# A graph layer on one Trainium2 core: degree factors folded into the matrix, and two tile pairs prepared during the counts

## The chip, the core and the metric

The kernel runs on one core of a Trainium2 chip. The core has five engines that run their own instruction queues and meet at semaphores: TensorE (matrix products from SBUF into PSUM), VectorE, ScalarE, GpSimd (SBUF only in this kernel) and SyncE, which issues the DMA transfers. The metric is the device time of one execution in microseconds, 912.77 us as the median of three runs (912.65 to 914.29).

## What is computed

`x` is 64 tiles of 128 rows (T) by 1024 nodes (N). The reference, cut to what matters (h = relu(layernorm(x)), n = 1024 nodes):

```python
x_avg = mean of h over the 64 tiles, per node;  x_norm = x_avg / |x_avg|
sim  = (x_norm @ x_norm.T + 1) * 0.5                       # n x n
adj  = (sim + gumbel0 > 1 - sim + gumbel1)                 # n x n, 0 or 1
adj_sym = clip(adj + adj.T, 0, 1); nmask = clip(adj_sym + eye, 0, 1)
common = nmask @ nmask.T;  max_common = common.max()
struct = where(adj_sym * (common > 1) > 0, common / max_common * common, 0)
W = adj * struct;  deg = W.sum(axis=0);  dinv = deg ** -0.5 (0 where deg is 0)
Wn = dinv[:, None] * W * dinv[None, :]
out = einsum('sd,sbt->dbt', Wn, einsum('nbt,to->nbo', h, weight)) + bias
result = x + out, transposed back to the layout of x
```

So the 64 tiles need one matrix Wn that depends on all of them, and then each tile is x + (h W) Wn + bias.

## The kernel before

**First pass (to about 110 us).** All 64 tiles are loaded, normalised and summed; of every eighth tile the product with W is kept (`xw_res`, tile RESIDENT = 0 of each trip).

**Setup (about 110 to 231 us).** TensorE makes sim, the symmetric mask, and the counts `common` in eight chunks of 128 rows, in the order of `CHUNKS`: chunk e of the upper half, then its partner of the lower half (L642 to L652, 16 matmuls each, three PSUM buffers `ps_com`). VectorE multiplies each with the adjacency into `masked[e]` (L859), the square root of W but for constants. ScalarE squares it into `a32(e)` (L426). The degrees are sums over rows of `a32` on TensorE (`degrees`, L618, matmuls one column wide). The matrix is wanted in seven combinations of its four 512 x 512 blocks for a Strassen-like product (Winograd's form, seven half-size products instead of eight), each split into a high and a low fp16 part (`a16[part, matrix 0 to 6]`): VectorE makes the combinations per chunk (`ts`, L812, and t3 on GpSimd, L353), ScalarE the high parts (`high_a`, `high_t`, L413 to L422), VectorE and GpSimd the low parts (L828 to L840, L363). The degree factors are not in `a16`: `dinv` goes into `u` (L899), by which z is multiplied, and into the row factor `row_fb` (L989), by which the results are multiplied. Only then are pair 0's tiles prepared.

**The loop.** 32 pairs of tiles, eight trips of four pairs (`act_pair`, `pe_pair`, `dve_pair`, and a GpSimd loop, L367). Tiles of a pair are the two halves (b = 0, 1) of the seven-product scheme. For the pair after next ScalarE makes h twice, fp32 and fp16 (`relu2`, L446 and L447), and VectorE the low fp16 part (`h_low`, L850). For the next pair TensorE makes h W (`xw_of`, L674, 24 matmuls a tile; the resident tile has none), VectorE turns it into z (`z_of`, L920, times u), GpSimd makes four sums of z (L370 to L375), ScalarE casts z and its sums in four groups to fp16 (`y_high`, L462), and VectorE subtracts for the low parts (`y_low`, L928). For the pair itself TensorE makes seven products of twelve matmuls of 512 columns (`product`, L683) in the order of matrices 0, 3, 4, 2, 5, 1, 6, in three PSUM banks (`ps_a`, `ps_b`, `ps_d`), reusing `ps_b` four times in a row as a running sum. Its intermediate states are copied out by ScalarE (`partial`, L476, four a pair) and combined on VectorE (L956, L962, L966), multiplied by the row factor and the weight's sum (`scale`, L932), and finished with bias and x (`finish`, L939). SyncE stores the tile and reloads its slot of `xring` (L277, L279).

The order on each engine is written by hand, and each engine is in order. In the loop ScalarE's order is: partial 0, y_high 0, partial 1, relu2, partial 2, y_high 1, relu2, y_high 2, partial 3, y_high 3. The last product, matrix 6, waits for partial 3:

```python
pe.wait_ge(s_v, 4 * r + 4)          # L707
product(q, 2, 6, ps_b, False)
```

## Time and profile before

| | |
|---|---|
| median of three runs | 912.77 us (912.65 to 914.29) |
| the profiled execution, its time | 917.18 us |
| its span, first to last instruction | 915.3 us |
| mean granted TensorE clock | 0.978 of full |
| DMA | 109.4 MB, mean 120 GB/s |

The profile names an instruction by engine, line of the kernel and operation, with output and inputs. PE is TensorE's matmul, PEld its weight load, DVE VectorE, ACT ScalarE, POOL GpSimd. An instruction's idle bracket is the time that its engine stood before it, and what released it. A busy TensorE is not TensorE at its peak: its matmuls overlap, so the starts of the runs of matmuls say more than the busy time. fp32 matmuls stand in the trace twice each. The granted clock is given as a share of 2.4 GHz; 0.5 is 1.2 GHz. Ends of matmuls are modelled, and GpSimd's spans are rough.

### The profile page before, as it was taken

The numbers are of one execution on the slowest core, as the hardware profiler recorded it, in microseconds if no ns is written. First come the engines' busy times: TensorE is split into PE (matmuls) and PEld (weight loads), VectorE is DVE, ScalarE is ACT, GpSimd is POOL, SyncE is SP. The second block draws the span as 40 slices with busy tenths as digits, with TensorE's granted clock in tenths as the row PEclk, the third lists the DMA queues.
The fourth block names the chain that finished last, engine by engine and source line by source line (L and its number), as shares of the span: only waits on it lengthen the run. The fifth ranks groups of instructions, "written<-read, shape, count | busy, mean of one in ns | idle before, by whom it ended". The sixth has DMA issues, their size and how long they took to land.

```text
span 915.3 us, 13816 instructions
## 1 busy us (share of the span) xinstructions
PE 846.0 (92%) x4772; PEld 435.1 (48%) x4772; DVE 748.9 (82%) x792; ACT 424.2 (46%) x472; POOL 336.9 (37%) x264
## 2 busy tenths in 40 slices
PE   5999899968999999999999999999999999999997
PEld 3444455654454445444444454444444444444453
DVE  7998666888888888888888888888888888888885
ACT  3888703455444443444344444444444444444431
POOL 4788511254333333333333333333334333433330
PEclk9999899868999999999999999999999999999999
DMA  8999600040222222222222232223222222222112
GB/s 351 409 399 401 278 1 1 1 184 1 92 93 93 92 92 92 92 92 92 106 94 94 94 135 89 98 94 113 92 92 92 92 92 92 92 92 92 47 47 92
DMA packets 29108, 109.40 MB, mean 120 GB/s; under 512 B 3360, under 2 KB 3488, under 8 KB 28064
## 3 DMA queue, kind: packets, MB, share of 16 engines
q1 hardware_dynamic: 29088, 109.13, 32.3%
q8 instruction: 13, 0.21, 0.1%
q14 instruction: 7, 0.06, 0.0%
HBM read 75.56 MB, written 33.55 MB: 119 GB/s over the span
## 4 chain that ended last, share of the span: by engine, by line
DVE 29%; issue 27%; PE 14%; ACT 14%; POOL 13%; DVEq 1%; ACTq 1%; POOLq 1%; DMA 0%; SPq 0%
DVE zbuf L920 8%; DVE obuf L932 7%; DVE obuf L962 5%; POOL zbuf L372 5%; ACT ybuf L462 4%; PE ps L683 4%; POOL zbuf L370 4%; PE ps L650 3%; ACT hring L447 3%; ACT hring L446 3%; DVE ybuf L928 2%; DVE obuf L966 2%; PE ps L555 2%; ACT p L476 1%; PE ps L626 1%
## 5 line engine op out<-in xcount | busy, mean ns | idle before, releaser
L683 PE MATMUL ps<-a,ybuf 128*128 128x512 f16 x2688 | 598.8, 380 | 36.3 <-ACT obuf L476 29.9
L683 PEld LDWEIGHTS ps<-a,ybuf 128*128 128x128 f16 x2688 | 256.6, 98 | 357.4 <-ACT obuf L476 50.5
L462 ACT ACTIVATE ybuf<-zbuf 128x1024 f16<-128x1024 f32 (+1 forms) x128 | 121.6, 950 | 333.3 <-DVE zbuf L920 227.8
L928 DVE TENSOR_TENSOR ybuf<-zbuf,ybuf 128x1024 f16<-128x1024 f32 (+1 forms) x128 | 190.0, 1484 | 60.3 <-ACT ybuf L462 60.3
L370 POOL TENSOR_TENSOR zbuf<-zbuf 128x512 f32<-128x512 f32 x32 | 41.5, 1296 | 455.3 <-DVE zbuf L920 455.3
L850 DVE TENSOR_TENSOR hring<-hring 128x1024 f16<-128x1024 f32 x56 | 73.3, 1308 | 51.3 <-ACT hring L447 51.3
L674 PE MATMUL ps<-w,hring 128*128 128x128 f16 x1344 | 85.5, 221 | 3.6 <-DVE hring L850 3.6
L674 PEld LDWEIGHTS ps<-w,hring 128*128 128x128 f16 x1344 | 79.6, 99 | 18.4 <-DVE zbuf L920 7.4
L476 ACT ACTIVATE obuf<-ps 128x512 f32<-128x512 f32 x96 | 56.2, 586 | 64.3 <-PE ps L683 64.3
L939 DVE SCALAR_TENSOR_TENSOR obuf<-obuf,bias_sb,xring 128x1024 f32<-128x1024 f32 x64 | 82.2, 1285 | 2.9
L375 POOL TENSOR_TENSOR zbuf<-zbuf 128x512 f32<-128x512 f32 x32 | 71.8, 2244 | 0.0
L373 POOL TENSOR_TENSOR zbuf<-zbuf 128x512 f32<-128x512 f32 x32 | 70.9, 2216 | 0.0
L446 ACT ACTIVATE hring<-xring,nbias,rstd 128x1024 f32<-128x1024 f32 x56 | 68.7, 1228 | 0.1
L447 ACT ACTIVATE hring<-xring,nbias,rstd 128x1024 f16<-128x1024 f32 x56 | 68.7, 1227 | 0.0
L920 DVE TENSOR_TENSOR zbuf<-ps,u 128x1024 f32<-128x1024 f32 x56 | 68.2, 1217 | 0.6 <-DVE hring L989 0.4
L932 DVE SCALAR_TENSOR_TENSOR obuf<-obuf,w_sum,hring 128x512 f32<-128x512 f32 x64 | 64.9, 1015 | 1.2
L962 DVE TENSOR_TENSOR obuf<-obuf,p 128x512 f32<-128x512 f32 x32 | 53.8, 1683 | 2.5 <-ACT obuf L476 2.5
L372 POOL TENSOR_TENSOR zbuf<-zbuf 128x512 f32<-128x512 f32 x32 | 51.8, 1620 | 2.5
L748 DVE BATCH_NORM_STATS2 stats<-xring 128x6 f32<-128x512 f32 x64 | 38.9, 671 | 0.7 <-issue 0.7
L748 DVE BATCH_NORM_STATS2 stats<-ybuf 128x6 f32<-128x512 f32 x56 | 34.2, 668 | 3.0 <-DMA ybuf<-in_x_dram 3.0
L555 PE MATMUL ps<-hring,ident 128*128 128x512 f32 x76 | 35.1, 609 | 0.0
L650 PE MATMUL ps<-xring 128*128 128x512 bf16 x128 | 30.7, 400 | 0.0
(142 smaller groups left out, 629.6 us busy)
## 6 DMA issues: line engine op xcount, KB each, us to landing
xring<-in_x_dram SPq DMA_DIRECT2D x96, 512.0 KB, 5.0
out_dram<-obuf SPq DMA_DIRECT2D x64, 512.0 KB, 3.0
ybuf<-in_x_dram SPq DMA_DIRECT2D x28, 512.0 KB, 9.7
a<-in_L_gnn_gumbel_dram SPq DMA_DIRECT2D x7, 1024.0 KB, 14.7
obuf<-in_x_dram SPq DMA_DIRECT2D x4, 512.0 KB, 11.8
...
bias_sb<-in_L_gnn_bias_dram SPq DMA_DIRECT2D x1, 0.5 KB, 2.1
```

Source lines behind the costliest of these rows:

```text
L370: nc.gpsimd.tensor_tensor(z[:, 4, :], z[:, 0, :], z[:, 3, :], ALU.add).then_inc(s_zs, 1)
L372: nc.gpsimd.tensor_tensor(z[:, 5, :], z[:, 4, :], z[:, 1, :], ALU.subtract).then_inc(s_zs, 1)
L446: nc.scalar.activation(h32, xring[:, j, :], ACT.Relu, bias=bias, scale=scale).then_inc(s_h32, 1)
L447: nc.scalar.activation(h16[b][:, 0, :], xring[:, j, :], ACT.Relu, bias=bias, scale=scale).then_inc(s_hhi, 1)
L462: nc.scalar.activation(y16[:, q % 2, 0, a:a + n, :], z[:, a + 1:a + 1 + n, :], ACT.Copy).then_inc(s_yhi, 1)
L674: mm = nc.tensor.matmul(ps_xw2[:, c * P:(c + 1) * P], h16[b][:, hk, c * P:(c + 1) * P], w16[:, wk, :], start=(hk == wk == 0), stop=(hk == ...
L683: mm = nc.tensor.matmul(bank[q % 2], y16[:, q % 2, yk, u, c * P:(c + 1) * P], a16[:, ak, mat, c, :], start=(start and c == yk == ak == 0), ...
L920: nc.vector.tensor_tensor(dst.rearrange("p m (c t) -> p m c t", c=HC), src, u[:].rearrange("p (m c) -> p m c", m=2).unsqueeze(3).broadcast_to(
L928: nc.vector.tensor_tensor(y16[:, q % 2, 1, a:a + n, :], z[:, a + 1:a + 1 + n, :], y16[:, q % 2, 0, a:a + n, :], ALU.subtract).then_inc(s_y, 1)
L932: return nc.vector.scalar_tensor_tensor(out=dst, in0=src, scalar=w_sum[:, 0:1], in1=row_fb[:, cols], op0=ALU.mult, op1=ALU.mult)
L939: nc.vector.scalar_tensor_tensor(out=ob, in0=ob, scalar=bias_sb[:, 0:1], in1=xring[:, j, :], op0=ALU.add, op1=ALU.add).then_inc(s_out, 1)
L962: nc.vector.tensor_tensor(o1[:, HI], o1[:, HI], p5[:], ALU.add).then_inc(s_c22, 1)
```

## The change

Both degree factors go into the matrix. As W is a square, the kernel makes `masked * q_row * q_column` with q = deg^(-1/4), and squares it: the square holds dinv on both sides. So z needs no `u` (a constant scale), and results no row factor. This needs the degrees before the matrix, so the matrix is no longer made chunk by chunk during the counts but after them, in whole blocks of 4 x 512 columns.

- Degrees: TensorE also transposes the adjacency, chunk by chunk (`turn_adj`), ScalarE copies it to SBUF (`turned`), VectorE makes a second, transposed mask of the same counts (`mask_t`), and ScalarE squares it with a sum along the row (`degree_of`). The degree matmuls are gone. GpSimd's powers of -1/4 come in two groups (`roots`, chunks 0 to 5 and 6 to 7).
- Two count buffers in PSUM instead of three.
- During the counts pairs 0 and 1 are prepared (relu2, xw_of, z, z_sums, y_high and most of y_low), from x tiles loaded into free buffers (`x_first`).
- After the counts q is spread over a row in PSUM (`ps_q`, `ps_q2`). VectorE multiplies the upper blocks' chunks (`rooted`), GpSimd the lower blocks' (`rows_lo`, from a copy of the row in SBUF); ScalarE squares all (`square`), with a scale that holds the constants (and for the lower blocks the column factor).
- z_of moves from VectorE to ScalarE. Three partial sums are copied by ScalarE with scale and bias (Identity), the fourth is read by VectorE directly (`upper1`). VectorE's combinations scale in the same pass (`upper0`, `upper1`, `lower0`, `lower1`) and `add_x` adds x.
- The first trip's pairs are written out ahead of the loops; product 6 of a pair waits for `upper1`.
- The loads of the first eight x slots wait for the end of the matrix (`s_t` 3, `s_alo` 5 and 6).

The diff, cut to its core and indented less (of `dve_pair`, at the end, only the lines that stay or come; `MADE` is (0, 3, 2, 4, 5, 1, 6), the order in which the matrices become ready):

```diff
-        sp.wait_ge(s_com, C)
-        sp.wait_ge(s_m, C)
-        for j in (1, 2, 3, 0, 4, 5, 6, 7):
+        sp.wait_ge(s_adj, C)
+        for k, j in enumerate((1, 2, 3)):
+            sp.dma_start(x_first[j], x[j]).then_inc(s_xf[k], 16)
+        sp.wait_ge(s_t, 3)
+        sp.wait_ge(s_alo, 5)
+        for j in (4, 5, 6, 7):
+            sp.dma_start(xring[:, j, :], x[j]).then_inc(s_x2[j], 16)
+        sp.wait_ge(s_alo, 6)
+        for j in (0, 1, 2, 3):
             sp.dma_start(xring[:, j, :], x[j]).then_inc(s_x2[j], 16)
...
+        def roots(n, a, b):
+            pool.wait_ge(s_degmin, 2 * n + 2)
+            nc.gpsimd.tensor_tensor(q_raw[:, a:b], degree_min[:, a:b], neg_quarter[:, a:b],
+                                    ALU.pow).then_inc(s_qraw, 1)
+        pool.wait_ge(s_cnt, 1)
+        nc.gpsimd.tensor_tensor(k0[:, 1:2], k0[:, 0:1], neg_half[:, 0:1], ALU.pow).then_inc(s_k0, 1)
+        z_sums(0)
+        roots(0, 0, 6)
+        z_sums(1)
+        roots(1, 6, C)
+        pool.wait_ge(s_qsb, 1)
+        for c in range(HC):
+            nc.gpsimd.tensor_tensor(rows_lo[:, c, :], masked[2 * c + 1], q_row, ALU.mult).then_inc(s_elo, 1)
+        pool.wait_ge(s_a32, C)
+        pool.wait_ge(s_t, 1)
+        nc.gpsimd.tensor_tensor(rows_hi[:, :, HI], rows_lo[:, :, HI], rows_hi[:, :, HI],
+                                ALU.subtract).then_inc(s_t3, 1)
+        with pool.Fori(2, TRIPS * PAIRS) as r:
+            z_sums(r)
...
+            dst = z[:, 1:3, :] if b == 0 else z[:, 0:4:3, :]
+            nc.scalar.activation(dst, src, ACT.Copy, scale=Y_SCALE / W_SCALE).then_inc(s_z, 1)
...
+                act.wait_ge(s_c, 4 * r + 6)
+            act.wait_ge(s_mm, 14 + 7 * r + (1, 2, 3)[k])
+            dst = (o[q % 2][0][:, 0:H], p5[:], o[q % 2][0][:, H:N])[k]
+            src = (ps_b, ps_d, ps_b)[k][q % 2]
+            nc.scalar.activation(dst, src, ACT.Identity, bias=bias_sb[:, 0:1],
+                                 scale=w_out[:, 0:1]).then_inc(s_v, 1)
...
         def act_pair(i, q, ahead1, ahead2):
             partial(i, q, 0)
             if ahead1:
+                z_of(i, q + 1, 0)
                 y_high(i, q + 1, 0)
             partial(i, q, 1)
             if ahead2:
                 relu2(i, q + 2, 0)
             partial(i, q, 2)
             if ahead1:
+                z_of(i, q + 1, 1)
                 y_high(i, q + 1, 1)
             if ahead2:
                 relu2(i, q + 2, 1)
             if ahead1:
                 y_high(i, q + 1, 2)
-            partial(i, q, 3)
-            if ahead1:
                 y_high(i, q + 1, 3)
...
+        def degree_of(e):
+            act.wait_ge(s_mt, e + 1)
+            if e >= 2:
+                act.wait_ge(s_deg, e - 1)
+            nc.scalar.activation(square_t[e % 2], masked_t[e % 2], ACT.Square,
+                                 accum_out=degree[:, e:e + 1]).then_inc(s_deg, 1)
...
+        turned(7)
+        degree_of(6)
+        degree_of(7)
+        y_high(0, 1, 2)
+        y_high(0, 1, 3)
+        act.wait_ge(s_qrow, 2)
+        act.wait_ge(s_deg, C)
+        nc.scalar.activation(q_row, ps_q2, ACT.Copy).then_inc(s_qsb, 1)
...
+        for c in range(HC):
+            square(rows_hi, 0, c)
+        act.wait_ge(s_a32, HC)
+        high(0, rows_hi[:, :, LO])
+        square(rows_lo, 1, 0)
+        square(rows_lo, 1, 1)
+        act.wait_ge(s_t, 1)
+        high(3, spare)
+        square(rows_lo, 1, 2)
+        square(rows_lo, 1, 3)
+        act.wait_ge(s_a32, C)
+        high(2, rows_lo[:, :, HI])
+        act.wait_ge(s_t, 2)
+        high(4, rows_hi[:, :, LO])
+        act.wait_ge(s_t3, 1)
+        high(5, rows_hi[:, :, HI])
+        high(1, rows_lo[:, :, LO])
+        act.wait_ge(s_wout, 1)
+        partial(0, 0, 0)
+        partial(0, 0, 1)
+        partial(0, 0, 2)
+        act.wait_ge(s_t, 3)
+        high(6, spare)
+        relu2(0, 2, 0)
+        relu2(0, 2, 1)
...
+        for e, c in enumerate(CHUNKS):
+            if e >= 2:
+                pe.wait_ge(s_m, e - 1)
+                pe.wait_ge(s_mt, e - 1)
+            for k in range(C):
+                if e == 0:
+                    for n in {c % 2, k % 2}:
+                        pe.wait_ge(s_mask[n], max(c, k) // 2 + 1)
+                if e >= 1 and k == HC:
+                    turn_adj(e)
+                for m in range(2):
+                    mm = nc.tensor.matmul(ps_com[e % 2][:, m * H:(m + 1) * H], nmask[:, k, c * P:(c + 1) * P],
+                                          nmask[:, k, m * H:(m + 1) * H], start=(k == 0), stop=(k == C - 1),
+                                          skip_group_check=True)
+            mm.then_inc(s_com, 1)
+            if e == 0:
+                turn(0)
+                turn_adj(0)
+            if e == 1:
+                spread(0)
+                xw_of(0, 0, 1)
+            if e == 3:
+                xw_of(0, 1, 0)
+            if e == 6:
+                xw_of(0, 1, 1)
+        pe.wait_ge(s_m, C)
+        turn(1)
+        pe.wait_ge(s_adjt, C)
+        for dst in (ps_q, ps_q2):
+            for c in range(C):
+                e = CHUNKS.index(c)
+                mm = nc.tensor.matmul(dst[:, c * P:(c + 1) * P], qf[:, e:e + 1].broadcast_to([P, P]), ident[:],
+                                      start=True, stop=True, skip_group_check=True)
+            mm.then_inc(s_qrow, 1)
+            if dst is ps_q:
+                spread(1)
...
-            pe.wait_ge(s_v, 4 * r + 4)
+            pe.wait_ge(s_c, 4 * r + 10)
+            made(6)
             product(q, 2, 6, ps_b, False)
...
+        root(0, 0, 6)
+        y_low(0, 1, 1)
+        bound(1, 6, C)
+        root(1, 6, C)
+        dve.wait_ge(s_q, 2)
+        nc.vector.tensor_reduce(col2[:, 1:2], qf[:], AX_X, ALU.max).then_inc(s_colmax, 1)
...
+        top_of(1)
+        y_low(0, 1, 2)
+        dve.wait_ge(s_qrow, 1)
+        rooted(rows_hi, 0, 0)
+        dve.wait_ge(s_topb, 2)
+        nc.vector.tensor_scalar(q_top[:], ps_top[1][:, P:P + 1], Q_MIN, None, ALU.max).then_inc(s_kap, 1)
+        rooted(rows_hi, 0, 1)
+        dve.wait_ge(s_kap, 1)
+        nc.vector.reciprocal(q_inv[:], q_top[:]).then_inc(s_kap, 1)
+        rooted(rows_hi, 0, 2)
+        dve.wait_ge(s_kap, 2)
+        dve.wait_ge(s_k0, 1)
+        nc.vector.tensor_scalar(kappa[:, 0:1], q_inv[:], k0[:, 1:2], A_SCALE ** 0.5, ALU.mult,
+                                ALU.mult).then_inc(s_kap, 1)
+        dve.wait_ge(s_cnt, 2)
+        nc.vector.tensor_scalar(w_out[:], q_top[:], q_top[:, 0:1], w_count[:, 0:1], ALU.mult,
+                                ALU.mult).then_inc(s_wout, 1)
+        rooted(rows_hi, 0, 3)
+        dve.wait_ge(s_kap, 3)
+        nc.vector.tensor_scalar(kappa_lo, qf[:].rearrange("p (c k) -> p k c", k=2)[:, 1, :], kappa[:, 0:1], None,
+                                ALU.mult).then_inc(s_kap, 1)
+        dve.wait_ge(s_a32, HC)
+        nc.vector.tensor_tensor(spare, rows_hi[:, :, HI], rows_hi[:, :, LO], ALU.subtract).then_inc(s_t, 1)
+        low(0, rows_hi[:, :, LO])
+        low(3, spare)
+        dve.wait_ge(s_a32, C)
+        dve.wait_ge(s_t, 1)
+        dve.wait_ge(s_alo, 1)
+        nc.vector.tensor_tensor(rows_hi[:, :, LO], rows_lo[:, :, HI], spare, ALU.subtract).then_inc(s_t, 1)
+        low(2, rows_lo[:, :, HI])
+        low(4, rows_hi[:, :, LO])
+        dve.wait_ge(s_t, 2)
+        dve.wait_ge(s_alo, 2)
+        nc.vector.tensor_tensor(spare, rows_lo[:, :, LO], rows_hi[:, :, LO], ALU.subtract).then_inc(s_t, 1)
+        low(5, rows_hi[:, :, HI])
+        low(1, rows_lo[:, :, LO])
...
+        def upper1(i, q):
+            r, ob = PAIRS * i + q, o[q % 2][1]
+            dve.wait_ge(s_mm, 14 + 7 * r + 5)
+            dve.wait_ge(s_v, 3 * r + 2)
+            nc.vector.scalar_tensor_tensor(out=ob[:, HI], in0=ps_b[q % 2], scalar=w_out[:, 0:1], in1=p5[:],
+                                           op0=ALU.mult, op1=ALU.add).then_inc(s_c, 1)
+        def add_x(i, q, b):
             j, ob = 2 * q + b, o[q % 2][b]
+            dve.wait_ge(s_c, 8 + 4 * (PAIRS * i + q) + 3 + b)
             dve.wait_ge(s_x2[j], 16 * (i + 1))
-            nc.vector.scalar_tensor_tensor(out=ob, in0=ob, scalar=bias_sb[:, 0:1], in1=xring[:, j, :],
-                                           op0=ALU.add, op1=ALU.add).then_inc(s_out, 1)
...
         def dve_pair(i, q, ahead1, ahead2):
             if ahead1:
                 y_low(i, q + 1, 0)
             if ahead2:
                 h_low(i, q + 2, 0)
             if ahead1:
                 y_low(i, q + 1, 1)
+            upper0(i, q)
             if ahead2:
                 h_low(i, q + 2, 1)
+            upper1(i, q)
             if ahead1:
                 y_low(i, q + 1, 2)
+            lower0(i, q)
+            add_x(i, q, 0)
             if ahead1:
                 y_low(i, q + 1, 3)
+            lower1(i, q)
+            add_x(i, q, 1)
...
+        upper0(0, 0)
+        low(6, spare)
+        upper1(0, 0)
+        y_low(0, 1, 3)
+        h_low(0, 2, 0)
+        lower0(0, 0)
+        add_x(0, 0, 0)
+        h_low(0, 2, 1)
+        lower1(0, 0)
+        add_x(0, 0, 1)
+        for q in range(1, PAIRS):
```

## Rows read from the trace of the kernel before

**Rows 1.** The page, busy time by engine over the whole span.

```profile
PE 846.0 (92%) x4772; PEld 435.1 (48%) x4772; DVE 748.9 (82%) x792; ACT 424.2 (46%) x472; POOL 336.9 (37%) x264
```

**Rows 2.** Timeline of PE, one pair: start us, duration us, instruction, count, idle bracket.

```profile
506.23 8.09 PE L683 MATMUL ps<-a,ybuf 128*128 128x512 f16 x36
515.64 5.35 PE L683 MATMUL ps<-a,ybuf 128*128 128x512 f16 x24 [1.32 <-ACT obuf L476]
520.83 1.50 PE L674 MATMUL ps<-w,hring 128*128 128x128 f16 x24
522.17 5.34 PE L683 MATMUL ps<-a,ybuf 128*128 128x512 f16 x24
527.35 1.50 PE L674 MATMUL ps<-w,hring 128*128 128x128 f16 x24
528.89 18.30 PE L683 MATMUL ps<-a,ybuf 128*128 128x512 f16 x84
```

**Rows 3.** Timeline of all engines in the same pair, ahead of the idle bracket.

```profile
509.68 1.22 DVE L920 TENSOR_TENSOR zbuf<-ps,u 128x1024 f32<-128x1024 f32 x1
...
512.41 1.61 POOL L372 TENSOR_TENSOR zbuf<-zbuf 128x512 f32<-128x512 f32 x1
...
512.80 0.68 DVE L956 TENSOR_TENSOR obuf<-ps,obuf 128x512 f32<-128x512 f32 x1
...
514.05 1.06 ACT L462 ACTIVATE ybuf<-zbuf 128x1024 f16<-128x1024 f32 x1 [0.23 <-POOL zbuf L372]
515.01 0.58 ACT L476 ACTIVATE obuf<-ps 128x512 f32<-128x512 f32 x1
515.13 2.22 DVE L928 TENSOR_TENSOR ybuf<-zbuf,ybuf 128x1024 f16<-128x1024 f32 x1
...
517.28 1.75 DVE L962 TENSOR_TENSOR obuf<-obuf,p 128x512 f32<-128x512 f32 x1
```

**Rows 4.** Timeline of PE, pair 0 and the start of pair 1.

```profile
212.29 7.72 PE L683 MATMUL ps<-a,ybuf 128*128 128x512 f16 x24 [4.00 <-DVE ybuf L928]
221.19 13.11 PE L683 MATMUL ps<-a,ybuf 128*128 128x512 f16 x60
```

**Rows 5.** Timeline of all engines, the end of the run.

```profile
880.81 28.65 PE L683 MATMUL ps<-a,ybuf 128*128 128x512 f16 x132
...
910.94 1.28 DVE L939 SCALAR_TENSOR_TENSOR obuf<-obuf,bias_sb,xring 128x1024 f32<-128x1024 f32 x1
```

**Rows 6.** Groups by line and form: busy us, mean ns of one | idle us before.

```profile
L462 ACT ACTIVATE ybuf<-zbuf 128x1024 f16<-128x1024 f32 x96 | 101.5, 1057 | 274.4 <-DVE zbuf L920 168.9 <-POOL zbuf L375 89.2 <-POOL zbuf L372 11.6
...
L446 ACT ACTIVATE hring<-xring,nbias,rstd 128x1024 f32<-128x1024 f32 x56 | 68.7, 1228 | 0.1
...
L932 DVE SCALAR_TENSOR_TENSOR obuf<-ps,w_sum,hring 128x512 f32<-128x512 f32 x32 | 23.9, 745 | 0.0
...
L422 ACT ACTIVATE a<-obuf 128x2048 f16<-128x2048 f32 x4 | 7.6, 1898 | 1.0 <-DVE obuf L823 1.0
...
L839 DVE TENSOR_TENSOR a<-obuf,a 128x2048 f16<-128x2048 f32 x2 | 4.6, 2291 | 2.4 <-ACT a L422 2.4
```

**Rows 7.** Timeline of PE in the setup: four of the counts, and the row factor's spread.

```profile
153.18 13.99 PE L650 MATMUL ps<-xring 128*128 128x512 bf16 x64
...
201.32 3.04 PE L536 MATMUL ps<-ident,row_f 128*128 128x128 f32 x16
```

**Rows 8.** Timeline of all engines after the counts, 189 to 200 us.

```profile
189.44 2.10 POOL L360 TENSOR_TENSOR dinv_raw<-degree,neg_half 128x8 f32<-128x8 f32 x1 [2.73 <-DVE has_deg L885]
...
191.51 6.14 POOL L363 TENSOR_TENSOR a<-obuf,a 128x1024 f16<-128x1024 f32 x2
...
194.53 4.20 DVE L850 TENSOR_TENSOR hring<-hring 128x1024 f16<-128x1024 f32 x1
```

**Rows 9.** Windows: busy us (instructions) by engine, then granted clock, DMA share, GB/s.

```profile
190.00:200.00 10.00, 2.17 (x15) 1.80 (x16) 9.24 (x13) 2.40 (x2) 7.64 (x3) 0.50 0.60 245
```

**Rows 10.** One line's instructions: durations in ns, first and last start in us.

```profile
L397 ACT ACT_TABLE_LOAD  x1: 1283/1283/1283, 0.8 to 0.8; - x1
```

More of the change, by code:

```diff
@@ L48 @@
 Y_SCALE = 256.0
+A_SCALE = 2.0 ** 14
+Q_MIN = 1e-6
 def gnn_kernel(nc, x, adj, bias, gumbel, out):
@@ L992, in _ @@
+            lower0(0, 0)
[3 more added lines that the diff above has]
+            add_x(0, 0, 1)
+            for q in range(1, PAIRS):
+                dve_pair(0, q, True, True)
+            with dve.Fori(1, TRIPS - 1) as i:
                 for q in range(PAIRS):
```

475 lines of the change are left out of this document (218 added, 257 removed).

## The prediction, made before the changed kernel was run

> **What bounds the kernel now.** I read the page's first part first [rows 1]: TensorE is busy 92% of the span, VectorE 82%, ScalarE and GpSimd under half. Busy time says little of a pipelined matmul, so the next view is TensorE's timeline in one pair of the steady loop [rows 2]. The reader is to see the starts there: 24 product matmuls from 515.64 to 520.83, 5.19 us, is 0.216 us each; the 24 matmuls of one tile's x·W take 1.34 us when nothing holds them (520.83 to 522.17). A pair of tiles has 84 product matmuls and two x·W, so it needs 18.14 + 2.68 = 20.82 us. It takes 22.66 us (506.23 to 528.89). The hole is at 515.64: TensorE stood 1.32 us for ScalarE's copy at L476, and 0.2 us more before each second x·W (1.54 instead of 1.34, 527.35 to 528.89) for VectorE's z. Of four pairs in a trip three have the hole.
>
> Which chain ends last at that hole is in the timelines of the other engines [rows 3]: VectorE writes z at 509.68, GpSimd's sums of z follow until 514.0, ScalarE's cast of that sum stands in its queue at 514.05, and only behind it, at 515.01, the copy of the fourth partial sum, on which product 6 of the pair waits (`s_v`, L707). The copy needs nothing of z; it is merely queued behind it. VectorE itself is late with z because it spends some 18 us of each pair's 22.
>
> Products are named here by their matrix, in the order 0, 3, 4, 2, 5, 1, 6 in which a pair runs them. So the loop has a price above TensorE's own work, and the setup ahead of it a long chain. Two anchors divide the run [rows 4, 5]. Five products run without a hole from 221.19 (60 matmuls); four belong to pair 0, so pair 1 starts at 221.19 + 48 x 0.216 = 231.5. The last matmul ends at 880.81 + 28.65 = 909.5, the last VectorE instruction at 910.94 + 1.28 = 912.2, the span at 915.3. The 31 pairs between take 678.0 us.
>
> **The loop.** Removed on VectorE: z_of (two of 1.22), the second reading of c22, three scalings by the row factor, the bias. Added: nothing; upper0, upper1 and lower0 scale and add in one pass from PSUM (0.75 each, by the same form of L932 [rows 6]), lower1 0.7, add_x twice 1.22 (the width of z_of in [rows 3]). y_low 4.3 and h_low 2.4 stay. I make it 12.1 us of own time instead of some 18 (82% of 22 [rows 1]), plus one to two us of standing behind GpSimd. Added on ScalarE: z_of twice, 1.0 us each from PSUM; the copy of the fourth partial sum (0.59) goes; the three others get a scale and a bias held in a column each, which in [rows 6] makes 1.228 of 1.057 for 1024 columns, so 0.17 each. The casts 3.8, four copies 2.3 and four relus 4.9 made 11.0; 11.0 + 2.0 - 0.6 + 0.5 = 12.9 us in 20.8, which still fits.
>
> What is late next? With product 0 of a pair starting at 0, x·W ends at 3.9, ScalarE has z at 5.2 and its cast at 6.2; the second x·W ends at 10.5, z at 11.7. GpSimd's four sums then take turns with VectorE's operations until 20.1, and the last cast is out at 21.2, ahead of the next pair's first copy at 23.4. VectorE reads product 5's sum (upper1) as soon as it ends, at 15.6, unless h_low is still before it: h_low waits for relu2, done at 14.7, and perhaps one GpSimd instruction, and ends at 15.9 to 16.5; upper1 then at 17.3 at the latest. Product 6 asks for it at 18.2. So I cost the loop at TensorE's own work, with 0.9 us to spare at the narrowest place. What is queued behind upper1's wait on VectorE is y_low of the next pair, not needed for 7 us. The loads and stores keep their places behind add_x; a result is stored 24 us after its pair's start and its buffer wanted at 44.
>
> Sum of the loop: 31 x 84 x 0.216 = 562.5, and 53 x·W (60 tiles of pairs 2 to 31 less 7 resident ones) at 1.34 = 71.0, together 633.5 against 678.0: **-44.5 us**. It can't gain more, since no matmul is taken away; it can gain less by what new waits arise, bounded by the old hole of 1.32 a pair.
>
> **The end.** The last block had a scaling and the addition behind it; now lower1 (0.7) and add_x (1.23), from 909.5: 911.5 instead of 912.2 [rows 5]. **-0.7 us**.
>
> **The setup.** I carry the time of the trace along. The counts start at 145.8 as before. TensorE now does there 8 counts at 3.46 us (64 matmuls in 13.8 [rows 7]), 8 transposes of eight 128-column matmuls (a third of an x·W, 0.45) and three x·W: 27.7 + 3.6 + 4.0 = 35.3, and with holes of 1.5 us (the two count buffers wait for both masks; I stepped VectorE's and ScalarE's queues through it) the counts end at 182.7. The masks are 16 passes of 1.22 from PSUM, ScalarE's new squares with a sum 1.1 each, its transposed copies 1.0. ScalarE is full there (34 us of work in 37), so this phase has hardly a reserve. That work moved here is what pair 0 and 1 cost before the loop earlier: z, casts and sums.
>
> Then the chain. Second mask and degree of the last chunk: 185.1. GpSimd has in its queue roots of six chunks, the four sums of pair 1 and only then the roots of the last two: sums from 183 to 189.5 (5.9 us alone), roots 0.8 (2.1 for eight columns [rows 8]), 190.3. Maximum, transposition: 191.2. The row of q, eight pieces at half clock: 3.0 [rows 7], 194.3. I take the half clock because TensorE stands here for 8 us, and in the same place of the trace, with 2.2 of 10 us busy, the granted clock was 0.50 [rows 9]. Four products with q on VectorE (1.15 apart) and seven small steps: 199.9. Four squares on ScalarE at 1.05: 204.1. From there VectorE has nine operations of 2048 columns at 2.2 apart (2.29 each alone [rows 6]) = 19.8 before low(1) is out. GpSimd has its last product with q (2.4) and the difference t3 (4.05) to do in the same stretch.
>
> These exclude each other: in [rows 8] VectorE's h_low, 1.22 alone, took 4.20, from 194.53 to 198.7, and ended 1.1 us after GpSimd's two instructions did (197.65), while in [rows 3] a pass that reads PSUM (L956) took its usual 0.68 at 512.80 in the middle of GpSimd's L372. So the four products of VectorE with q in PSUM are not slowed by GpSimd's four products, but the nine operations are: 204.1 + 1.7 (rest of a product) + 19.8 + 2.4 + 4.1 = 232.1. "SBUF — State Buffer" of the Trainium skill, section "Who interferes with whom", says the same of two SBUF inputs, and goes on that `tensor_scalar` and `copy` may enter a mode that takes the shared pair too. By that rule the steps for kappa (`tensor_scalar` on SBUF) would stand behind GpSimd's products, as no row here shows; the sum would be 1 to 2 us longer.
>
> TensorE's pair 0 walks behind: product 0 at 212.7, 3 at 219, and 4 at 227.4, not because of its matrix (225.6) but because ScalarE's copy of the first partial sum is queued behind four casts of 1.8 (until 226.6). Five products are left: 13.0 us at full clock, up to 16.8 at half clock (after the last stall of the trace 24 matmuls took 7.6 instead of 5.2 [rows 4]). Pair 1 starts at 240.4 to 244.2; I take 242. Its x tiles are loaded from 230.8 on, land in some 5 us, and are first needed at 244. Against 231.5: **+10.5 us**. From both sides: 236 if neither GpSimd nor the clock costs anything; 250 if the clock falls in the counts as well, twice at 3 us (estimated from those 24 matmuls).
>
> **The sum.** -44.5 - 0.7 + 10.5 = -34.7. The profiled execution took 917.2 with a span of 915.3; the span becomes 880.6. The median of the timed runs is 912.8, 4.4 under the profiled execution; I take the same difference off it: **878 us**.
>
> **Rivals.**
> A. The setup costs more: the phase in which ScalarE is full misses its steps (each transposed copy waits for the one before through one PSUM buffer), or the clock falls. For it: 34 of 37 us. Against: the waits in my stepping stayed under 2 us. 8 to 20 us on top: 886 to 898.
> B. A wait in the place of the one removed: product 6 now waits for upper1 on VectorE, which stands behind h_low and GpSimd. For it: VectorE's L928 and L962, 1.22 and 0.69 alone, took 2.22 and 1.75 beside GpSimd [rows 3]. Against: 0.9 us to spare. At 0.3 to 0.7 a pair: 887 to 900.
> C. Slower: `Identity` takes the place of `Copy` in three copies a pair. If it needed another table, ScalarE would load one at each change, six a pair. A load took 1.28 us [rows 10]; 7.7 + 12.9 = 20.6, and with the standing for GpSimd's sums, 89.2 / 32 = 2.8 ahead of the last cast [rows 6], about 23.4 a pair. It decides for slower from 21.55 a pair on ((678.0 - 9.8) / 31); at 23.4: 31 x 23.4 = 725.4, 47.4 more than before, with the other two terms 970 us. Against: Relu, Copy, Square and Sign share the kernel before, with one load in all. "ScalarE: Activation LUTs" of the Trainium skill, section "Table sets: the hidden batching unit", says that identity is in every set; by that C would not occur.
> D. The setup is better than bounded by my chain (pair 1 at or before 236): 866 to 872.
> That the change doesn't do what it says I see no room for: each removed instruction is gone from the code.
>
> **How the numbers follow.** Forecast 0.70 (872 to 886), A 0.11, B 0.09, C 0.03, D 0.07. 868 to 891 takes in the forecast, most of D and the near parts of A and B, and leaves out under 2 in 10. A measurement of this kernel tells about 0.2%, 1.8 us, from no change. C is slower; of A and B I put 0.01 each at no change and at slower, should both come at their worst: faster 0.95, same 0.01, slower 0.04.
>
> **What would show it.** TensorE's timeline in the loop: 60 or more product matmuls between x·W without an idle bracket, a trip of 4 x 18.14 + 7 x 1.34 = 82.0 us where it is 88.17 now. z written by ScalarE at 1.0 us. Pair 1's first product near 242; the roots behind z's sums on GpSimd; VectorE's nine operations ending near 232, some of them 4 us long. One ACT_TABLE_LOAD. Wrong if a trip is over 83, if TensorE stands before product 6 for VectorE, or if the counts end after 186.

## The result, and the profile after

The changed kernel takes 879.59 us (median of 4 runs, 877.91 to 880.53) against 912.82 us: a ratio of 0.9631 (95% interval 0.9613 to 0.9648), 33.2 us faster. Its profiled execution took 879.37 us with a span of 877.4 us. The page of the kernel after: busy time by engine, the chain that ended last, and the groups of the products, of z and of the copies with two column operands.

```profile
PE 824.6 (94%) x4756; PEld 430.9 (49%) x4756; DVE 577.2 (66%) x664; ACT 511.2 (58%) x524; POOL 329.6 (38%) x264
...
PE 80%; issue 6%; POOL 5%; DVE 4%; ACT 3%; POOLq 0%; DMA 0%; ACTq 0%; SPq 0%; DVEq 0%
...
L801 PE MATMUL ps<-a,ybuf 128*128 128x512 f16 x2688 | 592.5, 380 | 21.6 <-DVE a L1035 14.1
...
L501 ACT ACTIVATE obuf<-ps,bias_sb,w_out 128x512 f32<-128x512 f32 x64 | 49.5, 773 | 121.5 <-PE ps L801 121.5
...
L473 ACT ACTIVATE zbuf<-ps 128x1024 f32<-128x1024 f32 x56 | 57.3, 1023 | 21.5 <-PE ps L753 21.4
```

VectorE lost 172 us of busy time [rows 1], ScalarE gained 87. The second line is what matters. The same line of the kernel before is this one:

```profile
DVE 29%; issue 27%; PE 14%; ACT 14%; POOL 13%; DVEq 1%; ACTq 1%; POOLq 1%; DMA 0%; SPq 0%
```

There the chain ran through four engines and TensorE held 14% of it; now TensorE holds 80%. In the loop it never stands. TensorE's timeline after, one trip of four pairs, where [rows 2] had the bracket of 1.32:

```profile
515.97 18.29 PE L801 MATMUL ps<-a,ybuf 128*128 128x512 f16 x84
534.10 1.50 PE L753 MATMUL ps<-w,hring 128*128 128x128 f16 x24
535.44 13.11 PE L801 MATMUL ps<-a,ybuf 128*128 128x512 f16 x60
...
596.53 1.50 PE L753 MATMUL ps<-w,hring 128*128 128x128 f16 x24
597.87 2.32 PE L801 MATMUL ps<-a,ybuf 128*128 128x512 f16 x10
```

The trip is 597.87 - 515.97 = 81.9 us. Before it is 88.05 (the same runs of 84 matmuls start at 528.89, 616.92, 704.96 and 793.02); the prediction's 88.17 is a mean that takes in the first trip, of 88.42. The setup, timelines of all engines after (the counts end at 182.6, the two kinds of mask and the last degree follow):

```profile
187.99 0.70 POOL L384 TENSOR_TENSOR q_raw<-degree_min,neg_quarter 128x2 f32<-128x2 f32 x1
...
189.86 3.62 PE L791 MATMUL ps<-ident,qf 128*128 128x128 f32 x16
...
198.72 0.35 DVE L1057 TENSOR_SCALAR kappa<-qf,kappa 128x4 f32<-128x4 f32 x1
199.10 4.26 ACT L574 ACTIVATE xring<-xring,kappa 128x1024 f32<-128x1024 f32 x4 [2.27 <-DVE kappa L1057]
...
203.40 4.09 DVE L1060 TENSOR_TENSOR hring<-xring 128x2048 f32<-128x2048 f32 x1 [4.33 <-ACT xring L574]
...
211.59 4.68 POOL L398 TENSOR_TENSOR xring<-xring 128x2048 f32<-128x2048 f32 x1 [6.25 <-ACT xring L574]
211.82 6.60 DVE L1066 TENSOR_TENSOR xring<-xring,hring 128x2048 f32<-128x2048 f32 x1
...
218.45 5.51 ACT L579 ACTIVATE a<-xring 128x2048 f16<-128x2048 f32 x3 [4.99 <-DVE xring L1066]
```

and TensorE alone behind it, then the last run of products and VectorE's last instruction:

```profile
209.84 7.30 PE L801 MATMUL ps<-a,ybuf 128*128 128x512 f16 x24 [14.07 <-DVE a L1035]
224.68 17.09 PE L801 MATMUL ps<-a,ybuf 128*128 128x512 f16 x72 [7.54 <-ACT obuf L501]
241.60 1.50 PE L753 MATMUL ps<-w,hring 128*128 128x128 f16 x24
...
843.57 28.65 PE L801 MATMUL ps<-a,ybuf 128*128 128x512 f16 x132
```

```profile
873.11 1.23 DVE L1095 TENSOR_TENSOR obuf<-obuf,xring 128x1024 f32<-128x1024 f32 x1
```

Pair 1's product 0 is the last twelve of the 72 matmuls, so it starts at 241.60 - 12 x 0.216 = 239.0; before, 231.5. The matmuls end at 872.2. The sum of the span: loop 678.0 to 633.2 (-44.8), setup +7.5, end 5.8 to 5.2 (-0.6), together -37.9, as 877.4 - 915.3.

### The profile page after: what moved, and what is told of

The parts are those of the page before. It is cut to its first block, busy times and chain, and to the rows that moved or that the text cites. A ratio compares the mean times of both kernels' runs of the same rounds, so it can differ in the third digit from the quotient of the medians.

```text
span 877.4 us, 13592 instructions
## 1 busy us (share of the span) xinstructions
PE 824.6 (94%) x4756; PEld 430.9 (49%) x4756; DVE 577.2 (66%) x664; ACT 511.2 (58%) x524; POOL 329.6 (38%) x264
## 4 chain that ended last, share of the span: by engine, by line
PE 80%; issue 6%; POOL 5%; DVE 4%; ACT 3%; POOLq 0%; DMA 0%; ACTq 0%; SPq 0%; DVEq 0%
PE ps L801 66%; PE ps L753 8%; PE ps L657 2%; POOL rstd L339 1%; POOL zbuf L349 1%; ACT zbuf L414 1%; PE ps L682 1%; DVE xring L1066 1%; ACT xring L574 0%; DVE hring L1060 0%; ACT xw_res L419 0%; PE ps L633 0%; ACT a L579 0%; DVE xring L1029 0%; PE ps L696 0%
## 5 line engine op out<-in xcount | busy, mean ns | idle before, releaser
L801 PE MATMUL ps<-a,ybuf 128*128 128x512 f16 x2688 | 592.5, 380 | 21.6 <-DVE a L1035 14.1
L801 PEld LDWEIGHTS ps<-a,ybuf 128*128 128x128 f16 x2688 | 261.5, 98 | 328.9 <-issue 18.7
L960 DVE TENSOR_TENSOR ybuf<-zbuf,ybuf 128x1024 f16<-128x1024 f32 (+1 forms) x128 | 168.1, 1314 | 164.9 <-ACT ybuf L487 164.9
L501 ACT ACTIVATE obuf<-ps,bias_sb,w_out 128x512 f32<-128x512 f32 x64 | 49.5, 773 | 121.5 <-PE ps L801 121.5
L949 DVE TENSOR_TENSOR hring<-hring 128x1024 f16<-128x1024 f32 x56 | 68.6, 1224 | 59.5 <-ACT hring L459 59.5
L1095 DVE TENSOR_TENSOR obuf<-obuf,xring 128x1024 f32<-128x1024 f32 x64 | 78.4, 1224 | 2.8
L473 ACT ACTIVATE zbuf<-ps 128x1024 f32<-128x1024 f32 x56 | 57.3, 1023 | 21.5 <-PE ps L753 21.4
L459 ACT ACTIVATE hring<-xring,nbias,rstd 128x1024 f16<-128x1024 f32 x53 | 65.0, 1227 | 0.0
L501 ACT ACTIVATE p<-ps,bias_sb,w_out 128x512 f32<-128x512 f32 x32 | 24.8, 774 | 11.3 <-PE ps L801 11.3
L1100 DVE SCALAR_TENSOR_TENSOR obuf<-ps,w_out,obuf 128x512 f32<-128x512 f32 x32 | 24.0, 750 | 10.1 <-PE ps L801 10.0
L1080 DVE SCALAR_TENSOR_TENSOR obuf<-ps,w_out,obuf 128x512 f32<-128x512 f32 x32 | 23.6, 739 | 9.8 <-PE ps L801 9.8
## 6 DMA issues: line engine op xcount, KB each, us to landing
a<-in_L_gnn_gumbel_dram SPq DMA_DIRECT2D x7, 1024.0 KB, 15.7
```

The source lines that it names most:

```text
L459: nc.scalar.activation(h16[b][:, 0, :], src, ACT.Relu, bias=bias, scale=scale).then_inc(s_hhi, 1)
L501: nc.scalar.activation(dst, src, ACT.Identity, bias=bias_sb[:, 0:1], scale=w_out[:, 0:1]).then_inc(s_v, 1)
L801: mm = nc.tensor.matmul(bank[q % 2], y16[:, q % 2, yk, u, c * P:(c + 1) * P], a16[:, ak, mat, c, :], start=(start and c == yk == ak == 0), ...
L949: nc.vector.tensor_tensor(h16[b][:, 1, :], h32, h16[b][:, 0, :], ALU.subtract).then_inc(s_hlo, 1)
L960: nc.vector.tensor_tensor(y16[:, q % 2, 1, a:a + n, :], z[:, a + 1:a + 1 + n, :], y16[:, q % 2, 0, a:a + n, :], ALU.subtract).then_inc(s_y, 1)
L1095: nc.vector.tensor_tensor(ob, ob, xring[:, j, :], ALU.add).then_inc(s_out, 1)
```

## The experiments

### Which part of the change filled the hole

My reading in the prediction had two parts: VectorE's load made z late, and ScalarE's fourth copy queued behind the cast. The first part alone is theory L (load), the second alone theory Q (queues). The first three runs put things back in the changed kernel. The core of the first; the second has only the copy, the third only z:

```diff
 # ScalarE: z_of(i, q + 1, 0) and z_of(i, q + 1, 1) removed; VectorE has z_vec in the old places
+    partial3(i, q)        # ScalarE, behind y_high(.., 2): copies ps_b, as before the change
-            pe.wait_ge(s_c, 4 * r + 10)
+            pe.wait_ge(s_p3, r + 1)
```

> The changed kernel with two things of the loop undone, its matrix and its lighter scaling kept: z is made by VectorE again (by a constant), and the fourth partial sum is copied by ScalarE between the third and the fourth cast. Theory Q (queues): the hole of 1.3 us ahead of product 6 came from the fourth copy standing behind a cast of z's sums, and z standing behind h_low on VectorE. Both are back, so the hole is back: a trip of 86 to 88 us instead of 81.9, 910 to 925 us. Rival L (load): the hole came from VectorE's 18 us of work in a pair's 22; with some 14.5 us it stays away: trip 82 to 83, 880 to 887 us.

> The changed kernel with the fourth partial sum copied by ScalarE again, z stays on ScalarE. In the trace of the changed kernel the third cast ends at 540.9, product 5 at 540.6, and product 6 starts at 543.2; a copy between 540.9 and 541.7 is in time. Theory Q: no hole, trip 81.9 to 82.3, 878 to 883 us. Rival K (the place of the copy on ScalarE is enough for the hole): 1 to 1.3 us in three of four pairs, trip 85 to 86, 903 to 912 us. Rival L: as Q.

> The changed kernel with z made by VectorE again (by a constant), the fourth partial sum still read by VectorE. Theory Q: z and its sums come 1.2 us later, but product 6 no longer waits for them; it waits for upper1, which stands behind h_low and one more instruction of GpSimd and is due about when product 6 is: 0 to 0.3 us a pair, 880 to 889 us. Rival (z's place alone makes the hole): trip 85 to 88, 903 to 920 us.

Measured: 879.02 us (878.0 to 879.17), 878.24 (877.14 to 879.6) and 879.16 (878.14 to 879.81), beside 915.92 for the kernel before on the same chip. TensorE waits for nobody in the loop of any of the three. So the fourth copy behind the cast, which I had called the reason, can stand where it stood, and with z on VectorE as well. Q fell. With both put back the copy is out at 541.38 + 0.76 = 542.14 and product 6 due at 542.75: 0.6 us to spare. The third run came out below the 880 to 889 us that Q gave it. Of what is left, these three runs don't speak against L, since VectorE's lighter scaling is kept in all of them.

### z by ScalarE in the kernel before

```diff
+    nc.scalar.activation(dst, src, ACT.Copy, scale=Y_SCALE / W_SCALE)   # ScalarE, ahead of y_high
-    z_of(i, q + 1, 0)      # VectorE
-    z_of(i, q + 1, 1)
```

> The kernel before with only z moved to ScalarE, by a constant; the factor u is left out, so the source's degree factor is missing from the result. All else is as before, with the fourth copy and the row factor. Theory Q: z of the second tile is ready 1 us sooner, so the hole falls from 1.32 to 0.3 to 0.5 us, and the 0.2 us ahead of the second x·W go: trip 83.5 to 84.5 instead of 88.17, loop 28 to 36 us shorter, 877 to 885 us. Rival K: the hole stays at 1.1 to 1.3, trip 86.5 to 87.5, 900 to 908 us. Rival L: as Q, since VectorE loses 2.4 us a pair.

This kernel leaves out the factor u, so its result lacks one degree factor; it serves for the time alone. Measured: 869.73 us (868.68 to 870.57), ratio 0.9497, no wait of TensorE in the loop and a trip of 81.9 us. Better than the 877 to 885 us expected: all scalings still on VectorE, and still no hole. A load with so much left should have kept a part of it. So I looked for a ring of waits, which gives all or nothing. VectorE's timeline of the kernel before, around [rows 3], a pair earlier and a pair later (the cast between, L462, is ScalarE's):

```profile
508.53 1.23 DVE L850 TENSOR_TENSOR hring<-hring 128x1024 f16<-128x1024 f32 x1 [1.59 <-ACT hring L447]
...
519.73 0.68 DVE L966 TENSOR_TENSOR obuf<-ps,obuf 128x512 f32<-128x512 f32 x1
520.33 1.21 DVE L928 TENSOR_TENSOR ybuf<-zbuf,ybuf 128x1024 f16<-128x1024 f32 x1
521.46 1.28 DVE L932 SCALAR_TENSOR_TENSOR obuf<-obuf,w_sum,hring 128x1024 f32<-128x1024 f32 x1
522.77 1.28 DVE L939 SCALAR_TENSOR_TENSOR obuf<-obuf,bias_sb,xring 128x1024 f32<-128x1024 f32 x1
523.97 0.75 DVE L932 SCALAR_TENSOR_TENSOR obuf<-ps,w_sum,hring 128x512 f32<-128x512 f32 x1
524.75 1.28 DVE L939 SCALAR_TENSOR_TENSOR obuf<-obuf,bias_sb,xring 128x1024 f32<-128x1024 f32 x1
525.96 1.21 DVE L920 TENSOR_TENSOR zbuf<-ps,u 128x1024 f32<-128x1024 f32 x1
```

```profile
504.63 1.06 ACT L462 ACTIVATE ybuf<-zbuf 128x1024 f16<-128x1024 f32 x1 [5.76 <-DVE zbuf L920]
505.59 0.58 ACT L476 ACTIVATE p<-ps 128x512 f32<-128x512 f32 x1
506.07 1.23 ACT L446 ACTIVATE hring<-xring,nbias,rstd 128x1024 f32<-128x1024 f32 x1
507.20 1.23 ACT L447 ACTIVATE hring<-xring,nbias,rstd 128x1024 f16<-128x1024 f32 x1
```

The ring: y_low 2 starts at 515.13, as soon as its cast (out at 515.11) and the second h_low in VectorE's own queue let it, and from there VectorE works without a bracket through scale and finish to z at 525.96. ScalarE waits for that z (5.76 us of idle time in the row a pair earlier), casts it, copies p, makes h twice (507.20 to 508.43); h_low waits for that (508.53), z of the second tile is behind h_low (509.68), GpSimd's two sums follow, the cast at 514.05, and y_low 2 of the next pair at 515.13 again. That is 10.8 us on VectorE (515.13 to 525.96) and 11.8 us from z round to y_low 2, 22.66 in all, the period of three of the four pairs in a trip (the fourth, next to a tile whose x·W is kept, is shorter). The last stretch has two branches that end within 0.04 us of each other: beside GpSimd's sums, ScalarE's cast of the second z (510.93) and its next two passes for h (511.46, 512.60) lead to that second h_low, 513.92 to 515.15. Nothing in it waits for TensorE, and TensorE needs 20.82. Each round the ring is 1.84 us longer than TensorE's work; product 6 is only where TensorE meets it.

### The ring cut by order alone

If so, nothing need be taken off VectorE: it is enough to put z of the next tile ahead of 3.3 us of finish, scale and finish. In the kernel before, VectorE's queue alone is changed:

```diff
-    z_of(i, q + 1, 0)            # at the start of the pair, behind the last finish
 ...                             # scale of the first tile
+    if ahead2:
+        z_of(i, q + 2, 0)        # with which VectorE's next pair began, ahead of finish, scale, finish
```

> The kernel before with an order changed and nothing else: on VectorE z of the next pair but one's first tile stands ahead of the last three passes of a pair (finish, scale, finish: 1.28 + 0.75 + 1.28 us) instead of behind them. No work is removed or moved to another engine. Theory C (cycle): y_low 2, the passes up to finish, z, ScalarE's cast, relu2, h_low, z of the second tile, GpSimd's sums, the third cast and y_low 2 of the next pair form a ring of 22.66 us without TensorE in it, against TensorE's 20.82. 3.3 us less in the ring leave 19.4, TensorE bounds: trip 81.9 to 82.3 instead of 88.17, 866 to 873 us. Theory L (load: VectorE's 18 us of work in 22): nothing changes, 910 to 917 us. Theory Q (the fourth copy's place on ScalarE behind the sums of z): z of the second tile still stands behind h_low, most of the hole stays, 900 to 912 us.

Measured: 868.44 us (median of 5, 868.04 to 872.77), ratio 0.951 (0.9482 to 0.9537). TensorE's timeline and then VectorE's, of this kernel:

```profile
508.60 18.29 PE L683 MATMUL ps<-a,ybuf 128*128 128x512 f16 x84
526.73 1.50 PE L674 MATMUL ps<-w,hring 128*128 128x128 f16 x24
528.07 13.11 PE L683 MATMUL ps<-a,ybuf 128*128 128x512 f16 x60
```

```profile
540.23 1.28 DVE L932 SCALAR_TENSOR_TENSOR obuf<-obuf,w_sum,hring 128x1024 f32<-128x1024 f32 x1
542.56 1.22 DVE L920 TENSOR_TENSOR zbuf<-ps,u 128x1024 f32<-128x1024 f32 x1 [1.05 <-PE ps L674]
543.70 1.27 DVE L939 SCALAR_TENSOR_TENSOR obuf<-obuf,bias_sb,xring 128x1024 f32<-128x1024 f32 x1
```

No hole is left, and z now waits for TensorE (1.05), with the same instructions on every engine as before. VectorE is busy 72.9 us of a trip of 81.9, where it was busy 73.0 to 73.4 of 88: as much work in less time. The ring stands; L and Q, which wanted 900 us and more, are out. This kernel is faster than the kernel after as well, since it has the whole gain of the loop and its pair 1 starts at 231.6, as before the change. The smallest cut tried is these 3.3 us; no run took less than 1.84 us out of the ring, which would have shown whether the period follows its length.

### The slack ahead of product 6

In the kernel after, TensorE reads no copy there but waits for `upper1` on VectorE. All engines of the kernel after:

```profile
539.70 1.23 DVE L949 TENSOR_TENSOR hring<-hring 128x1024 f16<-128x1024 f32 x1 [0.39 <-ACT hring L459]
...
540.91 0.75 DVE L1088 SCALAR_TENSOR_TENSOR obuf<-ps,w_out,p 128x512 f32<-128x512 f32 x1
```

It ends at 541.66 and product 6 is due at 535.44 + 36 x 0.216 = 543.2: 1.5 us to spare where I had said 0.9. To see what it is worth, `upper1` was put behind the next y_low:

```diff
-                upper1(i, q)
                 y_low(i, q + 1, 2)
+                upper1(i, q)
```

> The changed kernel with upper1 behind y_low 2 on VectorE. In its trace upper1 ends at 541.7 and product 6 starts at 543.2; behind y_low 2 (1.22 to 2.2 us) it ends at 542.8 to 543.9. If 1.5 us are to spare, as this trace says: 0 to 0.3 us a pair, 879 to 888 us. If only the predicted 0.9 were: 0.4 to 1.0 a pair, 892 to 910 us.

Measured: 897.87 us (895.95 to 898.07), 18.3 more than the kernel after. The engines of this kernel:

```profile
528.37 2.30 POOL L378 TENSOR_TENSOR zbuf<-zbuf 128x512 f32<-128x512 f32 x1
...
529.54 2.21 DVE L960 TENSOR_TENSOR ybuf<-zbuf,ybuf 128x1024 f16<-128x1024 f32 x1
...
531.68 0.74 DVE L1088 SCALAR_TENSOR_TENSOR obuf<-ps,w_out,p 128x512 f32<-128x512 f32 x1
...
532.47 10.53 PE L801 MATMUL ps<-a,ybuf 128*128 128x512 f16 x48 [0.47 <-DVE obuf L1088]
```

The expectation failed: it had y_low at 1.22 to 2.2 us and `upper1`'s end as late as 543.9, 0.7 us behind product 6's turn, and yet priced that at 0 to 0.3 us a pair. y_low took 2.21 beside GpSimd's sum, so 1.5 us of slack was not enough, and the time lies in the range that I had given the other reading, of 0.9 us. The time alone can't tell the two apart; the 1.5 us stand on the rows of the kernel after. A second reading: the bracket says 0.47, but of the pair in hand 36 matmuls start at 544.18 and the next run at 552.59, 8.41 us, where 36 x 0.216 is 7.78. The pair loses 0.63. The hole of [rows 2] is 1.32 by its bracket and 515.64 - 506.23 - 7.78 = 1.63 by the starts. Of the difference 0.15 us is the modelled end of the run before (36 matmuls here last 7.93 where their starts take 7.78); in [rows 2] they last 8.09, so another 0.16 is lost inside that run. The bracket leaves out part of the loss: starts are what to count.

### What the setup costs, and what of it can be had back

Three things delay pair 1: the roots of the last chunks behind the sums of z on GpSimd (A), t3 on GpSimd while VectorE makes low(4) and so on (B), and ScalarE's copies of pair 0 behind three casts (C). All three together:

```diff
-            z_sums(1)
             roots(1)
+            z_sums(1)                                                # A
-            nc.gpsimd.tensor_tensor(rows_hi[:, :, HI], ...)          # B: to VectorE,
+            nc.vector.tensor_tensor(rows_hi[:, :, HI], ...)          #    behind low(4)
-            high(5, ...); high(1, ...)                               # C: two copies of
+            high(5, ...); high(1, ...)                               #    pair 0 ahead of them
```

> The changed kernel with three edits of its setup: GpSimd makes the last roots ahead of pair 1's sums; VectorE makes the difference t3 after low(4), so that GpSimd's 4.7 us no longer exclude it; ScalarE copies the first two partial sums ahead of two casts. Theory (my steps of the setup): the row of q 1 us earlier, t3 2.2 instead of 4.4 us on VectorE, product 4 at the end of low(4) instead of 1.9 us later; together 4 to 6 us earlier at pair 1's start: 873 to 876 us. Rival (the half clock and the loads of x bound pair 1's start): 0 to 1.5 us, 878 to 880 us.

> The changed kernel with one edit: on GpSimd the roots of the last two chunks stand ahead of pair 1's sums of z. In the trace of the changed kernel has_deg is ready at 186.9 and the roots come at 188.0 behind the sums. The row of q starts 1 to 2.5 us earlier: 877 to 879 us. Rival (another wait takes its place at once, y_low 2 with its cast, which stand ahead of the products with q): nothing, 879.6.

> The changed kernel with one edit: VectorE makes the difference t3 behind low(2), GpSimd no longer. Exclusion of the two engines: VectorE's L1066 took 6.60 instead of 2.28 behind GpSimd's 4.68; now 2.2 more work and 4.3 less standing: 2.1 us earlier, 877 to 878 us. Rival (the two share, no exclusion): VectorE's ten operations take longer than nine, 880 to 882 us.

> The changed kernel with one edit: ScalarE copies pair 0's first two partial sums ahead of the casts of matrices 5 and 1. Product 4 then waits for its matrix only (low(4) ends at 222.8 instead of the copy at 224.6): 1.9 us earlier, and what the half clock adds may follow: 875 to 878 us. Rival (the matrices 5, 1 and 6 set the end of pair 0): 0 to 0.5 us.

Measured: together 871.43 us (870.95 to 871.82), ratio 0.9532 (0.9511 to 0.9552), 8.2 less than the change as it is and more than the 4 to 6 expected. Alone: A 877.03 us (875.0 to 879.33), B 878.03 (877.24 to 878.96), C 876.96 (876.8 to 878.5), so 2.6, 1.6 and 2.6 less by the medians. None of the three is clear of noise: the kernel after itself lies from 877.91 to 880.53, e1 to e3, with the same setup, have medians of 878.2 to 879.2, and with C alone the row of q starts at 186.98 instead of 189.86, though C has no edit ahead of it. So their times came near what I expected, but not by what I expected.

Counted in each trace from the start of the row of q to pair 1's first product, the kernel after takes 49.2 us and the four others with its setup (e1, e2, e3, e6) 50.1 to 50.5; A takes 50.1, B 49.9, C 49.6, and all together 44.0. So behind the row of q none alone gives anything that these traces show: with B or A alone the copies are still late (TensorE's brackets of 5.22 and 7.16 end with ScalarE's copy), with C alone VectorE is. B did what it was for, the pass that takes VectorE 6.60 us at L1066 took 2.28, and another wait took its place. Ahead of the row of q, A saves 1.1 to 1.5 us: TensorE's bracket there is 5.59, with A alone and with all three, where the other kernels have 6.68 to 7.07. TensorE with C alone, and then with all three:

```profile
207.77 7.82 PE L801 MATMUL ps<-a,ybuf 128*128 128x512 f16 x24 [14.06 <-DVE a L1035]
220.90 18.44 PE L801 MATMUL ps<-a,ybuf 128*128 128x512 f16 x72 [5.31 <-DVE a L1035]
```

```profile
216.34 5.34 PE L797 MATMUL ps<-a,ybuf 128*128 128x512 f16 x24 [1.25 <-DVE a L1031]
222.94 5.34 PE L797 MATMUL ps<-a,ybuf 128*128 128x512 f16 x24 [1.27 <-ACT obuf L497]
228.58 5.35 PE L797 MATMUL ps<-a,ybuf 128*128 128x512 f16 x24 [0.29 <-DVE obuf L1086]
```

With C alone TensorE stands 5.31 us and its 72 matmuls then take 18.44, not 15.7: the granted clock of 220 to 230 us is 0.68. With all three no bracket behind the first 24 is above 1.27, the clock there is 1.00 and each 24 take 5.34. So each edit alone leaves one long stand of TensorE, and the half clock behind it; together they leave none. Which two of the three would do was not tried.

### TensorE kept busy while it stands

The half clock in the setup could be a cost of its own. On top of the three reorderings, matmuls of zeros were put into the places where TensorE stands:

```diff
+            pe.wait_ge(s_z, 4)
+            stay_awake(ps[:, 7, 2 * P:3 * P], 14)     # ahead of the row of q
+            stay_awake(ps[:, 7, 2 * P:3 * P], 42)     # behind it, ahead of product 0
```

> The reordered setup of e7 with small matmuls on zeros while TensorE stands: 14 after the counts, 42 after the row of q. If they hold the granted clock at full through the setup: the row of q takes 2.05 instead of 3.62 us, pair 0's first products 5.3 instead of 7.6 us, 1.5 to 3 us in all, 868.4 to 870 us, and a smaller spread. Rival (such matmuls don't hold it, or pair 0 waits for VectorE anyway): 871.4 us, with at most 1.5 of the row of q gained.

Measured: 870.8 us (869.1 to 871.71), 0.6 below the same kernel without them, less than the runs spread, and between the 868.4 to 870 of the expectation and its rival's 871.4. TensorE in this kernel:

```profile
187.14 2.76 PE L789 MATMUL ps<-ident,qf 128*128 128x128 f32 x16
...
192.76 9.54 PE L629 MATMUL ps<-ones,zeros 128*128 128x128 f32 x84
207.03 7.77 PE L799 MATMUL ps<-a,ybuf 128*128 128x512 f16 x24 [4.72 <-DVE a L1034]
```

The row of q takes 2.76 instead of 3.62. The mean clock is 0.991 instead of 0.985. The fillers end at 202.3, TensorE stands 4.72 us, and products 0 and 3 ran partly at half clock all the same (0.69 from 207 to 215 us, 24 matmuls in 7.77 instead of 5.34). What full clock there would give is not shown; I expect little, since the next products wait for VectorE (a bracket of 1.04).

### The kernel before once more

> The kernel before, unchanged, for a second profile of it. Its timed executions lie from 912.5 to 917.2, and the profile of before was the slowest of its kind at 917.2. If the spread comes from where the half-clock stretches fall in the setup, the loop's trip is 88.17 again and pair 1 starts up to 4 us from 231.5; if it comes from the loop, the trip differs.

Measured: 917.23 us, span 915.4, with the trip of 88.05 and the hole of 1.32 again. Its clock is 0.979, so this is another slow execution and no second kind. The timed executions of the same kernel beside it have spans of 910.7 us at 0.984, 912.3 at 0.982 and 914.2 at 0.980. In a span of 915 us a mean of 0.979 is 38 us at half clock (2 x 0.021 x 915), 0.984 is 29: nine us less at half clock, by this estimate up to 4.6 us of time. As the loop runs at 1.00, the setup or what is ahead of it holds the difference; no trace of a 910.7 us execution exists.

The profiles of the other kernels show one place. All have the same matmuls on TensorE up to the first count. At the end of the first pass TensorE stands 3 us for ScalarE in all of them. The rows behind it, and the first count, in the kernel after and then in e11:

```profile
108.95 3.78 PE L657 MATMUL ps<-obuf,ident 128*128 128x512 f32 x4 [3.03 <-ACT obuf L414]
...
145.84 3.62 PE L771 MATMUL ps<-xring 128*128 128x512 bf16 x16
```

```profile
108.94 1.98 PE L657 MATMUL ps<-obuf,ident 128*128 128x512 f32 x4 [3.05 <-ACT obuf L414]
...
142.96 3.62 PE L771 MATMUL ps<-xring 128*128 128x512 bf16 x16
```

The granted clock from 110 to 120 us is 0.76 in the first and 1.00 in the second. Over all 14 profiles it is 0.74 to 0.76 in four (before, e8, e5, after), with the first count at 145.8 to 146.0; 0.83 to 0.90 in eight, at 144.5 to 144.7; and 1.00 in two (e2, e11), at 143.0. So up to 3.0 us of a kernel's spread arise here. In e4, whose setup is that of the kernel before, the x·W behind the counts starts at 196.52 instead of 198.78: 1.1 us of that stem from this place and the rest from a second one, where the clock from 170 to 180 us is 1.00 instead of 0.69. Whether the 910.7 us execution differed at these two places alone is open.

## Why the prediction came out as it did

Predicted 878.0 us, measured 879.6, inside the range. Step by step:

- **The loop** (-44.5): -44.8. TensorE's own work was the right floor, and the trip of 82.0 is 81.9. z on ScalarE takes 1.02 us (said 1.0), copies with two column operands 0.77 (0.76), lower1 0.81 (0.7).
- **The reason for the hole** was wrong. "It is merely queued behind it" names the place where TensorE meets the ring. (The 0.2 us at the second x·W were misread too: TensorE stands behind that x·W, not ahead of it, and for ScalarE's copy of p; x·W itself starts on time, 24 x 0.216 us behind 522.17.) The sentence that fails is the one that priced VectorE's work as a sum of busy time; what set the pair was a loop of waits through VectorE, ScalarE and GpSimd, 22.66 us around. The forecast of the loop survived by luck of that kind: by the ring's length any cut over 1.84 us gives the full gain, and the change cuts far more. It would have failed for a smaller change: by my reading the reordering of e5 should have given little.
- **Rival B** had its place right. The slack was 1.5 us and not 0.9, because h_low took 1.23 beside GpSimd. What it costs once the slack is gone is shown by e6: 18.3 us, near the upper end I gave B (900).
- **The setup** (+10.5): +7.5. The counts (182.7) and the last degree (185.1) were met within 0.3. The last roots were out at 188.7 (said 190.3). The row of q started at 189.86 (said 191.2) and ran mostly at half clock as said, 3.62 us for its 16 (said 3.0; 2.05 for the second row behind it). The last square was out at 203.4 (204.1). The nine operations ended at 229.4, not 232.1: beside the earlier start I had added 1.7 + 2.4 + 4.1 = 8.2 us for GpSimd, two products and t3, and the trace shows 6.1. VectorE met only the end of one product (4.09 for 2.28, so 1.8), and t3 (6.60 for 2.28, so 4.3). Product 4 of pair 0 came at 224.7 (said 227.4), for the reason given, the copy behind the casts.
- **The end** (-0.7): -0.6.
- **From the span to the median** is the step that was unsound. I carried "4.4 us under the profiled execution" over as a constant. It is what one execution of the kernel before had above the others, and the changed kernel's profiled execution equals its median within 0.2. The span came out 3.2 us better than forecast (877.4 for 880.6), and from there to the median it went up 2.2 us instead of down 2.5, 4.7 worse; the total is off by only 1.6 because the two offset each other, which was luck. The median it starts from moves too: the kernel before stands at 912.8, 915.9, 914.2 and 915.1 us beside the four groups of runs.
- **Rival C** is out: one table load in the kernel after, 1.28 us, with Identity in three copies a pair. The Trainium skill ("ScalarE: Activation LUTs", section "Table sets: the hidden batching unit") puts identity in every set, and the trace agrees.
- The Trainium skill ("SBUF — State Buffer", section "Who interferes with whom") would have the small kappa step (`tensor_scalar`) stand behind GpSimd. In the kernel after it took 0.35 us (L1057), in other runs up to 1.32 (e10), and in each it ended 0.02 to 0.03 us after GpSimd's first product with q. Another `tensor_scalar`, L979 on two columns, took 1.23 us and ended at 186.83, where GpSimd's sum ended at 186.81; L980 behind it took 0.15. The runs agree with the page; the price of the kappa step is about 1 us at most, and in the kernel after less than the 1 to 2 us given for it.
